# A state space layer's opening: earlier loads of its powers, transposes moved ahead of the rows, and a copy moved from VectorE to ScalarE

## The reference, cut to what matters

```python
# first layer, end: 2 of 8 experts per row, and a shared expert
x = x + gb * _L0_ffn_ref(h, ...)
# second layer, beginning
h = _layernorm(x, axis=-1) * (1 + ca) + sa
x = x + ga * _L1_attn_ref(h, in_W, in_b, log_dt, C, log_A_real, A_imag, D_skip, ...)

def _L1_attn_ref(x, ...):
    x_in = x @ in_W.T + in_b
    u = jnp.swapaxes(x_in, 1, 2)
    dtA = A * dt[:, None]                                # A: 128 channels x 32 complex states
    K = jnp.exp(dtA[:, :, None] * jnp.arange(Lseq))      # the powers
    k = 2.0 * jnp.einsum('hn,hnl->hl', Ceff, K).real
    y = causal_convolution(u, k) + u * D_skip[:, None]   # written with an FFT in the reference
    y = gelu(y)
    z = jnp.einsum('oh,bhl->bol', glu_W, y) + glu_b[None, :, None]
    ...
    return out + x
```

## Time and profile before

| | |
|---|---|
| median of 3 runs | 1263.59 us (1256.02 to 1265.23) |
| profiled execution: time | 1261.72 us |
| profiled execution: span | 1260.2 us |
| TensorE (matmul), busy | 962.0 us, 76% |
| VectorE, busy | 830.9 us, 66% |
| ScalarE, busy | 695.9 us, 55% |
| GpSimd, busy | 444.4 us, 35% |
| mean granted TensorE clock | 0.868 of full speed |

### The profile page before, as it was taken

One profiled execution on the slowest core, in us unless ns is written; L12 is line 12 of the kernel. 1 busy time (PEld: TensorE's weight loads), 2 busy tenths in 40 slices (PEclk: granted clock), 3 DMA queues, 4 the chain that ended last, 5 costly groups with the idle time before them and its releaser, 6 DMA issues. The chain is left out here.

```text
span 1260.2 us, 26930 instructions
## 1 busy us (share of the span) xinstructions
PE 962.0 (76%) x9019; PEld 631.0 (50%) x9019; DVE 830.9 (66%) x2082; ACT 695.9 (55%) x1479; POOL 444.4 (35%) x510
## 2 busy tenths in 40 slices
PE   4565899999999999957748977827578446779990
PEld 2232343333434333445436766727455336779990
DVE  6797998999999999376523445447867444323445
ACT  3684477877877777734324555528024333446660
POOL 5617122323212221216652356520001462664441
PEclk9795699999999999966779989868778657999995
DMA  7236011111111100021111122257552321222226
GB/s 208 67 110 226 7 61 53 51 35 49 53 38 36 46 8 2 2 72 61 45 53 33 43 78 77 69 195 228 137 149 64 87 71 31 63 76 69 66 57 208
DMA packets 101694, 97.16 MB, mean 77 GB/s; under 512 B 15181, under 2 KB 85928, under 8 KB 101560
## 3 DMA queue, kind: packets, MB, share of 16 engines
q1 hardware_dynamic: 87320, 75.29, 20.2%
q0 software_dynamic: 8704, 17.97, 4.2%
q10 hardware_dynamic: 5536, 2.18, 0.6%
HBM read 60.18 MB, written 34.95 MB: 75 GB/s over the span
## 5 line engine op out<-in xcount | busy, mean ns | idle before, releaser
L569 DVE TENSOR_REDUCE part<-sps 128x2 f32<-128x1024 f32 (+2 forms) x307 | 327.5, 1114 | 27.1 <-PE sps L557 15.3
L912 ACT ACTIVATE prob<-tpa 128x1024 f32<-128x1024 f32 (+1 forms) x208 | 192.8, 927 | 45.2 <-PE tpa L858 43.3
L1738 POOL DMA_INDIRECT yk<-yo,place x144 | 146.7, 1019 | 179.4 <-ACT yo L1767 162.0
L744 POOL TENSOR_SCALAR_AFFINE_SELECT prob<-prob 128x512 f32<-128x512 f32 x128 | 80.5, 641 | 307.2 <-ACT prob L912 307.2
L1245 POOL DMA_INDIRECT xg<-h,slot x128 | 127.7, 998 | 130.6 <-DVE slot L1396 88.9
L878 PE MATMUL ops<-prob,vs 128*32 128x512 f32 (+3 forms) x1536 | 157.9, 498 | 0.1
L912 ACT ACTIVATE prob<-tpb 128x512 f32<-128x512 f32 (+1 forms) x224 | 126.8, 566 | 36.5 <-PE tpb L858 36.4
L1795 DVE COPY place<-xt 128x1 uint32<-128x1 uint32 x144 | 22.1, 153 | 187.9 <-ACT esg L1761 97.4
L550 PE MATMUL sps<-qk 48*128 48x512 bf16 (+2 forms) x734 | 132.4, 338 | 12.6 <-DVE part L569 7.8
L1858 PE MATMUL banks<-xT,y 128*128 128x128 f32 x864 | 112.9, 282 | 21.2 <-ACT y L1752 13.9
L1858 PEld LDWEIGHTS banks<-xT,y 128*128 128x128 f32 x864 | 105.7, 197 | 24.9 <-ACT xT L1747 17.8
(11 more groups left out here) (356 smaller groups left out, 1878.7 us busy)
## 6 DMA issues: line engine op xcount, KB each, us to landing
xt<-xg SPq DMA_DIRECT2D x144, 65.0 KB
qk<-term SPq DMA_DIRECT2D x24, 256.0 KB, 2.7
qk<-qk SPq DMA_DIRECT2D x64, 96.0 KB
arena<-kpad SPq DMA_DIRECT2D x6, 1024.0 KB, 11.0
powers<-powr SPq DMA_DIRECT2D x8, 516.0 KB, 5.3
powr<-powers SPq DMA_DIRECT2D x4, 1032.0 KB, 9.0
qk<-qk SPq DMA_DIRECT2D x64, 64.0 KB
h<-yk SPq DMA_DIRECT2D x8, 512.0 KB, 7.3
```

Source lines behind the costliest of these rows:

```text
L569: return nc.vector.tensor_reduce(to, src, AX.X, ALU.max, negate=True)
L744: nc.gpsimd.affine_select(out=blk, in_=blk, pattern=[[0, HQ], [1, P]], compare_op=ALU.is_ge, fill=0.0, base=0, channel_multiplier=-1).then ...
L912: nc.scalar.activation(prob[:, at:at + len(units), 0:n], slot_of(t, m)[:, :, 0:n], ACT.Exp, scale=float(HD) ** -0.5).then_inc(exp_done, 1)
L1738: nc.gpsimd.indirect_dma_start(out=d.yk, out_offset=bass.IndirectOffsetOnAxis(ap=place[:, u:u + 1], axis=0), in_=yo[u][:], in_offset=None) ...
```

## The change

Seven edits:

1. SP issues the powers' loads as eight loads of 516 KB in the first layer's slot loop, at slots 46, 48, ... 60, instead of four at the head of the state space block. They go to `w.powr4`, a part of a buffer `w.pair` which before held only the layers' `h` copies for the scatter (those of layer 0 have been read by slot 40).
2. `combine(0)`, `combine(1)`, `statistics(0)` move from the end of the first layer's block to the head of VectorE's list in the state space block.
3. The sums' loads 4 to 6 land in a buffer of their own, `w.room`, and `norm(b)` no longer waits for `combine(b + 4)`; only `norm(3)` waits, for all of them. `room` later holds `h_c`, `q` and `y_odd`.
4. All eight `turn(n)` stand first in TensorE's list, and all eight `turned(n)` first in ScalarE's.
5. `inputs_out(s)` goes from VectorE to ScalarE, as a plain copy. The bias is put into PSUM by a product of the identity with the bias row, repeated four times (128x512), ahead of each `project(s)`, which adds to it.
6. ScalarE's list is, for each b: `root(b), norm(b), transposed(2b), transposed(2b+1), inputs_out(2b), inputs_out(2b+1)`.
7. `norm(b)` signals after 4 tiles and after 8, and `transpose(s)` waits for its own half.

```diff
+POWERS_AT = 46
@@ experts_parts, sync_part
             if TAILS_AT <= n < TAILS_AT + NE:
                 routed.tail(sp, n - TAILS_AT)
+            if layer == 0 and n >= POWERS_AT and n % 2 == 0 and n < POWERS_AT + 2 * (NG // GI):
+                w.first.powers(sp, (n - POWERS_AT) // 2)
@@ first_sum
-    gat = [flat[s // 4][:, s % 4 * 2 * ST:(s % 4 + 1) * 2 * ST] for s in range(2 * NB)]
+    w.room = ctx.enter_context(nc.sbuf_tensor("room", [P, 3 * 2 * ST], F32))
+    at = lambda a, n: a[:, n * 2 * ST:(n + 1) * 2 * ST]
+    gat = [at(flat[0], s) for s in range(4)] + [at(w.room, n) for n in range(3)] + [at(flat[1], 3)]
...
+    def powers(sp, n):
+        gs = slice(n * GI, (n + 1) * GI)
+        sp.dma_start(w.powr4[:, :, gs, :], d.powers[:, :, gs, :]).then_inc(w.p_in, 16)
@@ layer_phase, vector
-                if layer == 0:
-                    w.first.combine(dve, 0)
-                    w.first.combine(dve, 1)
-                    w.first.statistics(dve, 0)
-                else:
+                if layer == 1:
                     combined.vector(dve)
@@ s4_core, sync
-                for k in range(4):
-                    powers_in(k)
                 for n in range(4):
                     matrix_in(n)
@@ s4_core, vector
-                AHEAD, BEHIND = ([2], [5], [6], []), ([3, 4], [], [7], [])
+                combine(dve, 0)
+                combine(dve, 1)
+                statistics(dve, 0)
                 for b in range(NB):
-                    for s in AHEAD[b]:
-                        combine(dve, s)
+                    if b + 1 < NB:
+                        combine(dve, 2 * b + 2)
                     shifts(b)
-                    for s in BEHIND[b]:
-                        combine(dve, s)
                     if b + 1 < NB:
+                        combine(dve, 2 * b + 3)
                         statistics(dve, b + 1)
-                    (the eight inputs_out, which stood here and behind the loop)
@@ s4_core, scalar
                 def norm(b):
                     act.wait_ge(shifted, b + 1)
-                    act.wait_ge(x_done, b + 5)
+                    if b == NB - 1:
+                        act.wait_ge(x_done, 2 * NB)
                     for t in range(b * TPB, (b + 1) * TPB):
                         ins = nc.scalar.activation(h[:, t, :], w.x[:, t, :], ACT.Identity, ...)
-                    ins.then_inc(norm_done, 1)
+                        if t % 4 == 3:
+                            ins.then_inc(norm_done, 1)
+
+                def inputs_out(s):
+                    act.wait_ge(u_ps, s + 1)
+                    if s == 0:
+                        act.wait_ge(x_done, 4)
+                    dst = u_all.rearrange("p c t -> p t c")[:, 4 * s:4 * s + 4, :]
+                    nc.scalar.copy(dst, bank[:, 2 + s % 2, :].rearrange("p (j c) -> p j c", j=4)).then_inc(u_out, 1)
...
-                root(0)
-                norm(0)
+                for n in range(NI):
+                    turned(n)
                 for b in range(NB):
-                    if b + 1 < NB:
-                        root(b + 1)
-                    transposed(2 * b)
-                    transposed(2 * b + 1)
-                    if b + 1 < NB:
-                        norm(b + 1)
-                    turned(2 * b)
-                    turned(2 * b + 1)
+                    root(b)
+                    norm(b)
+                    for s in (2 * b, 2 * b + 1):
+                        transposed(s)
+                    for s in (2 * b, 2 * b + 1):
+                        inputs_out(s)
@@ s4_core, tensor
                 def project(s):
-                    pe.wait_ge(hT_done, s + 1)
                     after(pe, u_out, s - 1)
                     out = bank[:, 2 + s % 2, :]
+                    nc.tensor.matmul(out..., m.ident[:], inb[:]....to_broadcast([P, 4, C]), start=True, stop=False, ...)
+                    pe.wait_ge(hT_done, s + 1)
                     for j in range(4):
-                        ins = nc.tensor.matmul(out[:, j * C:(j + 1) * C], hT[s % 2][...], inT[:], start=True, stop=True)
+                        ins = nc.tensor.matmul(out[:, j * C:(j + 1) * C], hT[s % 2][...], inT[:], start=False, stop=j == 3, ...)
                     ins.then_inc(u_ps, 1)
...
+                for n in range(NI):
+                    turn(n)
                 for b in range(NB):
                     transpose(2 * b)
                     transpose(2 * b + 1)
                     project(2 * b)
-                    turn(2 * b)
                     project(2 * b + 1)
-                    turn(2 * b + 1)
```

More of the change, by code:

```diff
@@ L1907, in combine_parts @@
     sem = lambda n: semaphore_of(nc, ctx, n)
-    gat = [w.h[s // 4][:].rearrange("p t c -> p (t c)")[:, s % 4 * 2 * ST:(s % 4 + 1) * 2 * ST] for s in range(2 * NB)]
+    gat = [w.pair[:, s * 2 * ST:(s + 1) * 2 * ST] for s in range(2 * NB)]
     got = [sem(f"got{s}") for s in range(2 * NB)]
@@ L1947, in first_sum @@
     flat = [a[:].rearrange("p a b c -> p (a b c)") for a in (w.v, w.y)]
-    gat = [flat[s // 4][:, s % 4 * 2 * ST:(s % 4 + 1) * 2 * ST] for s in range(2 * NB)]
+    w.room = ctx.enter_context(nc.sbuf_tensor("room", [P, 3 * 2 * ST], F32))
+    at = lambda a, n: a[:, n * 2 * ST:(n + 1) * 2 * ST]
+    gat = [at(flat[0], s) for s in range(4)] + [at(w.room, n) for n in range(3)] + [at(flat[1], 3)]
+    w.p_in = sem("p_in")
     got = [sem(f"got4{s}") for s in range(2 * NB)]
@@ L1971, in first_sum @@
     made.load, made.combine, made.statistics, made.x_done, made.var_done = load, combine, statistics, x_done, var_done
+    made.powers = powers
     return made
@@ L2333, in s4_core @@
         sem = lambda n: semaphore_of(nc, ctx, n)
-        powr = sb("powr4", [P, 2, NG, LW])
+        powr = w.powr4
         arena = sb("arena", [P, 2, NG * LW])
         vr = sb("vr", [P, NI, 2, GI, P])
-        h_c = sb("h_c", [P, NG, 2, NT])
+        h_c = w.room[:, 0:NG * 2 * NT].rearrange("p (g a t) -> p g a t", g=NG, a=2)
         s_all, h_all = sb("s_all", [P, TPB, NG, 2, NB]), sb("h_all", [P, TPB, NG, 2, NB])
-        q = sb("hq", [P, 2, NG, 2, NB])
-        y_odd, shift = sb("y_odd", [P, ST]), sb("shift4", [P, NT])
+        q = w.room[:, NG * 2 * NT:NG * 2 * NT + ST].rearrange("p (k g a b) -> p k g a b", k=2, g=NG, a=2)
+        y_odd, shift = w.room[:, NG * 2 * NT + ST:NG * 2 * NT + 2 * ST], sb("shift4", [P, NT])
         bank = ctx.enter_context(nc.psum_tensor("s4_banks", [P, 8, ST], F32))
@@ L2352, in s4_core @@
         hT = [hflat[:, u * ST:(u + 1) * ST] for u in range(2)]
-        yl = [x.rearrange("p (g l) -> p g l", g=GI) for x in (q[:].rearrange("p k g a b -> p (k g a b)"), y_odd[:])]
+        yl = [x.rearrange("p (g l) -> p g l", g=GI) for x in (q.rearrange("p k g a b -> p (k g a b)"), y_odd)]
         i_step, r_step = sem("i_step"), sem("r_step4")
@@ L2357, in s4_core @@
         s_ps, s_out, hc_done = sem("s_ps4"), sem("s_out4"), sem("hc_done")
-        p_in, root_done = [sem(f"p_in{k}") for k in range(4)], sem("c_root")
+        root_done = sem("c_root")
         x_done, var_done, combine, statistics = w.first.x_done, w.first.var_done, w.first.combine, w.first.statistics
@@ L2369, in matrix_in @@
                     sp.dma_start(tz[n], src).then_inc(tz_in[n], 16)
-                def powers_in(k):
-                    gs = slice(2 * k * GI, 2 * (k + 1) * GI)
-                    sp.dma_start(powr[:, :, gs, :], d.powers[:, :, gs, :]).then_inc(p_in[k], 16)
-                for k in range(4):
-                    powers_in(k)
                 for n in range(4):
@@ L2414, in into_x @@
                     return v.tensor_tensor(xs, xs, h[:, 4 * s:4 * s + 4, :], ALU.add)
[L2416 to L2420, removed]
                 def states_out(n):
@@ L2537, in transpose @@
                 def transpose(s):
-                    pe.wait_ge(norm_done, s // 2 + 1)
+                    pe.wait_ge(norm_done, s + 1)
                     after(pe, hT_done, s - 1)
@@ L2545, in project @@
                 def project(s):
-                    pe.wait_ge(hT_done, s + 1)
                     after(pe, u_out, s - 1)
                     out = bank[:, 2 + s % 2, :]
+                    nc.tensor.matmul(out.rearrange("p (j c) -> p j c", j=4), m.ident[:],
+                                     inb[:].rearrange("p (o c) -> p o c", o=1).to_broadcast([P, 4, C]), start=True, stop=False, skip_group_check=True)
+                    pe.wait_ge(hT_done, s + 1)
                     for j in range(4):
-                        ins = nc.tensor.matmul(out[:, j * C:(j + 1) * C], hT[s % 2][:, j * C:(j + 1) * C], inT[:], start=True, stop=True)
+                        ins = nc.tensor.matmul(out[:, j * C:(j + 1) * C], hT[s % 2][:, j * C:(j + 1) * C], inT[:], start=False, stop=j == 3,
+                                               skip_group_check=True)
                     ins.then_inc(u_ps, 1)
                 def turn(n):
-                    pe.wait_ge(p_in[n // 2], 16)
+                    if n == 0:
```

(5 more changed lines are left out.)

## The result

The changed kernel takes 1273.15 us (median of 7 runs, 1269.97 to 1274.55); the kernel before, run beside it, takes 1260.95 us (7 runs, 1253.37 to 1265.23). The ratio is 1.0091, with a 95% interval of 1.0065 to 1.0116: slower, by 11.5 us going by the ratio and by 12.2 going by the medians. That is about the 1% that the forecast called its bound: the ratio lies inside it, the upper end of its interval outside. The forecast was 1273 us.

A forecast was written before the change was run, and what follows sets the result against it. The prediction took ScalarE to bound the opening of the state space block. Its terms, -0.8 + (37.1 - 30.8) + 0.1 + 6.0 = +11.6 us on the profiled 1261.72, gave 1273 us, range 1264 to 1281.

The forecast's parts named there:

- The serial list: State space batches: ScalarE starts nothing of batch b + 1 before batch b's copies are out, so parts add to 9.45 us.
- The first norm, 0.8 us gained: Opening of the state space block: first norm starts at 851.6 instead of 852.36, after block change and turns.
- The clock in the batches, 6.0 us: TensorE pauses 3.2 us in each batch, the clock falls, and 1.5 us is lost four times.
- the earlier of the two cases in the forecast: TensorE in each batch: clock back after 3.2 us rather than 6.4, 1.6 us exposed at half speed, 0.8 us lost.
- The scattered copy: ScalarE's second copy of a batch from PSUM to scattered addresses: 0.87 us, from 0.50 plus 0.37 for the target.
- TensorE's five terms of a batch: From the norm's end: second transpose 0.9, identity product 0.86, projection 0.9, identity product 0.86, projection 1.06 us.
- C: Rival for the batches: the clock holds at full speed, so only +5.6 us, total 1267.3; chance 0.17.
- the loads: Powers' loads in the first layer's slot loop: priced at nothing; up to 10 us if each were exposed in full.
- Lifting the wait for the sum: First norm no longer waiting for a VectorE sum: worth 4.1 us, not collected because the turns take its place.
- Rival B: Turns on TensorE: transposes don't raise the clock, all 64 take 13.4 us, +3.5 us more, 1276.8; chance 0.15.
- Rival D: Batches: hand-overs hide and ScalarE's own work bounds, 6.6 us a batch, 26.4 in all, total 1256.6; chance 0.10.
- E: Rival in the first layer's slot loop: the powers' loads delay slots, up to 10 us on top, 1283; chance 0.08.

The follow-up runs named there:

- experiment 1: Changed kernel with only ScalarE's list put back into its old overlap, root, transposes and norm of batch b+1 ahead of batch b's copies: ratio 0.9996 to the kernel before.
- experiment 4: Changed kernel with three unused 128x512 products on TensorE in the pause ahead of batches 1 to 3: ratio 1.0091 to the kernel before.
- experiment 9: Kernel before with only the powers' loads moved to slots 46 to 60 of the first layer: ratio 0.9993 to the kernel before.
- experiment 8: Kernel before with only the sums' loads 4 to 6 in their own buffer and norms not waiting for sum b + 4: ratio 0.9974.

## Why the prediction was right, step by step

- **The serial list** was the mechanism, and it is shown by experiment 1. A batch at the full clock was put at 9.45 us and measured at 9.47 (experiment 4), though with three unused products in its pause.
- **The first norm, 0.8 us gained**: this term failed, though small. It came 2.6 us later than before. The step "SP's last sum load is issued by 837.6; with 1.3 us for the change of block the lists begin at 838.9" left out GpSimd's drain. The turns began at +9.1, not +5.3: 3.1 of these 3.8 us are the drain's, and TensorE began 1.8 us behind the block's end, not 1.3. The turns' own length was right, 10.35 us for 10.6.
- **The clock in the batches, 6.0 us**: right in sign, too large. It cost 0.9 us a batch (10.4 against 9.47; the last, 9.90 against 9.05), some 3.7 in all, if the first batch, which was never run at the full clock, lost as much as the second. The clock fell in every batch, but in the second it was back 3.4 us after the transposes began, near the earlier of the two cases in the forecast. The norm had ended 1.9 us before that, so only those 1.9 us ran at half speed in the open.
- **The scattered copy**: taken at 0.87 us. A record is 1.02 us, of which 0.82 passes before the root starts, so that the sum was right.
- The two misses, 3.4 us too little at the first norm and 2.1 us too much behind it, nearly cancel: the states moved by 12.9 us where 11.6 were forecast. That the total was hit better than its terms is luck.
- **Two side figures** don't follow from the forecast's own terms. TensorE's five terms of a batch come to 4.6 us, so a clock that never rises would cost that, not 4.1, a batch. And with a copy at 0.50 us, C gives 1265.8 and not 1264, because only the second copy of a batch is in the open. Neither enters the sum; the second is the lower end of the range.
- **Priced at nothing**: the loads, rightly (experiment 9), and VectorE's relief, which no run took alone. Lifting the wait for the sum was put at 4.1 us uncollected; alone it brings 4.2 at the first norm and 2.3 at the states (experiment 8).
- **Rival B**, that transposes don't raise the clock, is refuted: from 838.76 TensorE did nothing but transposes, after 13 us without work, and at about 842.75 the clock went to 2.4 GHz. The Trainium skill ("TensorE: Matmul & The Clock Gate", Part 4: PE-mode transpose) says that the full clock doesn't engage for them. This trace says otherwise, and the measurement decides.
- **Rival D** would have been right for another list: experiment 1's first three batches, 6.2 to 7.0 us, are its 6.6 within 0.4. The last, with no norm to overlap, took 9.7, so from the first norm to the states are 29.9 us and not 26.4. It was refused because the list lets nothing overtake, and that was so. C, the clock holding, is refuted by the stretches above, E by experiment 9.

## What to carry to other kernels

When an engine that is the bound takes over another's work, look at where in its list the work stands before looking at its duration: a hand-over to another engine and back is free while the next batch's work stands between its two halves, and fully paid when it doesn't. Work moved across a barrier changes what ends the barrier; read the drains of all engines there, not the last thing that one queue issued. And an engine that waits for a barrier is the place for work that needs nothing from behind it.

## What the runs showed of the hardware that I had not expected

- GpSimd's drain at its last indirect scatters took 10.58 us in the changed kernel, 11.03 before and up to 11.32 in the experiments (experiment 1). SP's own wait for the same scatters had ended over 7 us before the drain did. Why it is so long wasn't tried.
- Adding 2.7 us of unused products to a pause of 3.2 us kept the granted clock at 1.0 and shortened a batch by 0.9 us.
- Transposes alone brought the clock from 1.2 to 2.4 GHz (begun at 838.76, at the full clock from about 842.75).
- ScalarE's copy of 128x512 from PSUM took 1.02 us into addresses 128 bytes apart and, where it stood alone, 0.59 us into neighbours; VectorE's copy into the same scattered target took 1.05.
- The same kernel took 1155.6 us on one chip and 1255 to 1261 on others. In the stage studied the traces agree within some 0.7 us (with the list unchanged up to there, the turns start at +9.06 to +9.08 on either, the first norm at +21.3 to +22.0). About half of the 100 us lies ahead of the first sum load (775.4 us in experiment 1's trace, 829.7 in the changed kernel's) and half behind the states (328.1 against 376.2); why wasn't looked into.
